# Attention and last feed-forward put into one block, with the first token blocks, the first products and the first gates rearranged

## The chip, the cores and the metric

The kernel runs on one core of a Trainium2 chip. The metric is the time of one execution on the device in microseconds, lower is better. Engines that run side by side, each in its own program order: TensorE (PE: matmuls and transposes), VectorE (DVE), ScalarE (ACT), GpSimd (POOL), and SyncE (SP), which here only issues DMAs. They wait for each other by semaphores. TensorE reads from SBUF and writes to PSUM, which has 8 banks of 2 KB per partition.

## What is computed

2048 tokens (16 blocks of 128) of width 256 go through two layers, each an attention and a feed-forward with a residual and a tanh gate. The change is in the second layer:

```python
x = x + tanh(g_xattn[1]) * L1_xattn(layernorm(x), ctx, ctx)      # 16 heads of 16, causal, 128 keys per block
x = x + tanh(g_ffn[1]) * L1_ffn(layernorm(x))

def L1_ffn(xf):                       # D = 256, hidden 128, E = 32 experts, 8 groups
    s = sigmoid(xf @ Wr.T + br)
    # best 4 of 8 groups by the sum of their top 2, then the best 6 experts in them
    w = s[idx] / sum(s[idx]) * 2.5    # the gates, 0 for the other experts
    moe = sum over e of gate[:, e] * (square(relu(xf @ W1[e].T)) @ W2[e].T)
    shared = square(relu(xf @ Ws1.T)) @ Ws2.T    # hidden 256
    return shared + moe
```

## The kernel before

Each phase is a block of its own (`nc.Block()`), with one program per engine and a barrier at its end. The change touches the last two: the attention (lines 1253 to 1456) and the call of `feed_forward` with tag "f1" (line 1458), which shares its code with the first layer's feed-forward "f0" (`gated` is true there).

**Precision.** Products are made of fp32 numbers split in two: `hi` is a rounded copy (ScalarE), `lo` the rest (a subtraction on VectorE or GpSimd), and a product is three matmuls (hi hi, hi lo, lo hi) for each half of 256: six matmuls of 128x512.

**The attention** has 64 steps n, four for each of the 16 token blocks b (t = n % 4 is the head group). TensorE's order in a step: `turned(n)` (four transposes of the shifted scores, line 1320), `scores(n + 2)` (three matmuls), `values(n)` (line 1331), and in some steps `query_turned` or `out_rows(b - 1)` (four transposes, line 1340). ScalarE: `out_copy` at t = 0, `probs(n)` (the exponential of what `turned` wrote), `query_copy`, `key_hi(n + 4)`, `query_normed`, `query_hi`. VectorE: `maxima(n + 1)`, `shifted(n + 1)`, and per block `inverse`, `scaled`, `residual` (line 1422), `moments`. GpSimd: `key_lo`, `query_lo`, a few small operations. `row_bank` (bank 7) and `x_bank` (bank 3) each serve one user at a time.

**The last feed-forward** has 34 weight units (2 shared, 32 experts), gone through twice (p = 0, 1), each time for two token blocks of 512 (s = 0, 1): 136 units K. Unit K's steps are `h_prod(K)` (TensorE, line 1017), `hidden(K)` (relu, ScalarE), `square(K)`, for experts `squared_y(K)` (times the gate row, VectorE, line 904), `y_hi(K)` (ScalarE, line 791), `y_lo(K)` (VectorE, line 880), `o_prod(K)` (TensorE, line 1046). TensorE's order is `h_prod(K + LA)`, `o_prod(K)` with LA = 2; ScalarE's `hidden(K)`, `y_hi(K - 1)`, `square(K)`; VectorE's `y_lo(K - 1)`, `squared_y(K)`, and `w_lo` every second unit. `h_prod` uses banks K % 3, `o_prod` adds up in banks 4 to 7.

Before its first product the block prepares token blocks m = 0 and 1: `normed` (VectorE), `transposed` (TensorE, line 1056), `x_hi`, `x_lo`, `logits_t` (router product, line 1065), its copy, `logits` (line 1072), `logits`' bias addition; `keep_clock` (line 110) fills TensorE meanwhile with 10 and 12 matmuls that nobody reads. Then come `sigmoid(0)` with a table load (ScalarE) and the routes `gates_of(0)` (VectorE, some 50 small operations from line 1219 to 1247), given out in three portions a unit before unit 3. `GATES_T` and `GATES_COPY` say at which unit TensorE turns the gates (`gates_t`, line 1080) and ScalarE copies them; SP stores them in DRAM (`store_gates`, line 724) and loads each expert's row back, spread over 128 partitions (`gate_rows`, line 720), into four slots G. Units 0 to 3 are shared and need no gate.

## Time and profile before

| | us |
|---|---|
| median of 3 runs | 973.37 |
| lowest, highest | 971.01, 975.56 |
| the profiled execution | 974.85 |
| its span in the profile | 972.7 |
| TensorE busy in it | 921.6 (95%) |
| VectorE, ScalarE, GpSimd busy | 603.9, 521.9, 190.1 |

The attention's steps run from about 417 to 544 us, the last feed-forward from 546 to the end. A timeline row gives the start, the duration, engine and line, output <- inputs, shapes, and in brackets how long the engine had been idle and who released it. Equal neighbouring instructions are merged (x4). The chain of waits is the path that ended last: each piece begins where what it waited for had ended.

### The profile page before, as it was taken

The numbers are of one execution on the slowest core, as the hardware profiler recorded it, in microseconds if no ns is written. First come the engines' busy times: TensorE is split into PE (matmuls) and PEld (weight loads), VectorE is DVE, ScalarE is ACT, GpSimd is POOL, SyncE is SP. The second block draws the span as 40 slices with busy tenths as digits, with TensorE's granted clock in tenths as the row PEclk, the third lists the DMA queues.
The fourth block names the chain that finished last, engine by engine and source line by source line (L and its number), as shares of the span: only waits on it lengthen the run. The fifth ranks groups of instructions, "written<-read, shape, count | busy, mean of one in ns | idle before, by whom it ended". The sixth has DMA issues, their size and how long they took to land. (4 is left out here: it accounts for less than half of the span.)

```text
span 972.7 us, 14048 instructions
## 1 busy us (share of the span) xinstructions
PE 921.6 (95%) x4776; PEld 733.5 (75%) x4776; DVE 603.9 (62%) x1411; ACT 521.9 (54%) x939; POOL 190.1 (20%) x162
## 2 busy tenths in 40 slices
PE   6799889999999999989999787999999999999997
PEld 5799768877788888756666655778788888888886
DVE  6677654455554565488888654565855556565554
ACT  3222043434443335468887344667666766666665
POOL 5899300000000002057787100000000000000000
PEclk8899999999999999999999898999999999999999
DMA  8100020332211432025554104444445344544443
GB/s 303 51 1 1 29 86 17 104 100 90 93 49 51 141 131 60 17 98 180 182 171 153 56 13 152 134 130 135 137 130 147 108 130 133 151 138 145 148 123 116
DMA packets 58535, 105.43 MB, mean 108 GB/s; under 512 B 7360, under 2 KB 13888, under 8 KB 58080
## 3 DMA queue, kind: packets, MB, share of 16 engines
q1 hardware_dynamic: 57744, 104.39, 33.9%
q8 instruction: 39, 0.64, 0.3%
q14 instruction: 32, 0.26, 0.1%
q10 hardware_dynamic: 720, 0.14, 0.1%
HBM read 102.08 MB, written 2.42 MB: 107 GB/s over the span
## 5 line engine op out<-in xcount | busy, mean ns | idle before, releaser
L880 DVE TENSOR_TENSOR ylof<-yf,yhif 128x512 fp32r<-128x512 f32 x200 | 138.2, 691 | 175.8 <-ACT yhif L791 175.4
L1017 PE MATMUL bank<-xhf,whif 128*128 128x512 f32 x528 | 212.4, 402 | 1.5 <-ACT rf L766 1.5
L1017 PE MATMUL bank<-xlf,whif 128*128 128x512 f32 x528 | 208.7, 395 | 0.0
L1017 PE MATMUL bank<-xhf,wlof 128*128 128x512 f32 x528 | 208.5, 395 | 0.0
L791 ACT ACTIVATE yhif<-yf 128x512 fp32r<-128x512 f32 x200 | 125.6, 628 | 89.3 <-DVE yf L893 82.5
L1046 PE MATMUL bank<-yhif,whif 128*128 128x512 f32 x400 | 160.0, 400 | 12.8 <-DVE ylof L880 12.7
L1046 PE MATMUL bank<-yhif,wlof 128*128 128x512 f32 x400 | 158.1, 395 | 0.0
L1046 PE MATMUL bank<-ylof,whif 128*128 128x512 f32 x400 | 157.2, 393 | 0.0
L768 ACT ACTIVATE rf<-bank 128x512 f32<-128x512 f32 x136 | 81.2, 597 | 124.7 <-PE bank L1017 123.9
L1017 PEld LDWEIGHTS bank<-xhf,whif 128*128 128x128 f32 x528 | 99.6, 189 | 24.5 <-ACT rf L766 1.9
L1017 PEld LDWEIGHTS bank<-xhf,wlof 128*128 128x128 f32 x528 | 99.7, 189 | 23.9
L1017 PEld LDWEIGHTS bank<-xlf,whif 128*128 128x128 f32 x528 | 99.8, 189 | 21.7
L1046 PEld LDWEIGHTS bank<-yhif,whif 128*128 128x128 f32 x400 | 75.4, 188 | 34.6 <-DVE ylof L880 18.1
L904 DVE TENSOR_TENSOR yf<-tf,Gf 128x512 f32<-128x512 f32 x128 | 87.6, 684 | 10.1 <-DMA Gf<-gates 10.1
L505 POOL TENSOR_TENSOR k_blocks_lo<-k_blocks_sb,k_blocks_hi 128x512 fp32r<-128x512 f32 x64 | 82.1, 1286 | 57.2 <-ACT k_blocks_hi L501 56.6
L1046 PEld LDWEIGHTS bank<-yhif,wlof 128*128 128x128 f32 x400 | 75.5, 189 | 18.1
L1046 PEld LDWEIGHTS bank<-ylof,whif 128*128 128x128 f32 x400 | 75.4, 189 | 17.2
L780 ACT ACTIVATE tf<-rf 128x512 f32<-128x512 f32 x128 | 79.5, 621 | 0.0
L766 ACT ACTIVATE rf<-bank 128x512 f32<-128x512 f32 x64 | 38.2, 597 | 75.8 <-PE bank L1017 75.7
L875 DVE TENSOR_TENSOR wlof<-wrawf,whif 128x512 fp32r<-128x512 f32 (+1 forms) x100 | 77.0, 770 | 1.3 <-ACT whif L759 1.3
L759 ACT ACTIVATE whif<-wrawf 128x512 fp32r<-128x512 f32 (+1 forms) x100 | 69.1, 691 | 0.7 <-DMA wrawf<-in_wu 0.7
L137 POOL TENSOR_TENSOR rstd<-vpe,mhalf 128x8 f32<-128x8 f32 (+2 forms) x8 | 13.2, 1648 | 243.2 <-DVE vpe L130 243.2
(133 smaller groups left out, 1215.4 us busy)
## 6 DMA issues: line engine op xcount, KB each, us to landing
Gf<-gates SPq DMA_DIRECT2D x160, 256.0 KB, 3.7
wrawf<-in_wu SPq DMA_DIRECT2D x68, 256.0 KB, 2.6
k_blocks_sb<-in_k_blk SPq DMA_DIRECT2D x64, 256.0 KB, 4.1
wrawf<-in_wu SPq DMA_DIRECT2D x32, 384.0 KB, 3.1
v_slot<-in_v_rows SPq DMA_DIRECT2D x16, 256.0 KB, 2.7
ctx_windows<-in_ctx_win SPq DMA_DIRECT2D x3, 1024.0 KB, 10.8
toeplitz<-in_kpad SPq DMA_DIRECT2D x4, 512.0 KB, 8.9
X<-in_x SPq DMA_DIRECT2D x4, 512.0 KB, 9.2
```

What stands on the lines that cost most here:

```text
L137: pool.tensor_tensor(rstd[:, bs], vpe[:, bs], mhalf[:, bs], ALU.pow).then_inc(done, 1)
L505: pool.tensor_tensor(K2[:, n % KR, :], KM[:, n % KLR, :], K1[:, n % KR, :].bitcast(F32), ALU.subtract).then_inc(s_k2, 1)
L759: act.activation(whi[:, Nu % S, :], wraw[:, Nu % S, :], ACT.Copy).then_inc(s_wh, 1)
L766: act.activation(r[:, K % S, :], bk(2 * K % 3), ACT.Silu).then_inc(s_ac, 1)
L768: act.activation(r[:, K % S, :], bk(K % 3), ACT.Relu).then_inc(s_ac, 1)
L780: act.activation(t[:, K % S, :], r[:, K % S, :], ACT.Square).then_inc(s_sq, 1)
L791: act.activation(yhi[:, K % S, :], y[:, K % S, :], ACT.Copy).then_inc(s_yh, 1)
L875: dve.tensor_tensor(wlo[:, Nu % S, :], wraw[:, Nu % S, :], whi[:, Nu % S, :].bitcast(F32), ALU.subtract).then_inc(s_wo, 1)
L880: dve.tensor_tensor(ylo[:, K % S, :], y[:, K % S, :], yhi[:, K % S, :].bitcast(F32), ALU.subtract).then_inc(s_yl, 1)
L904: dve.tensor_tensor(y[:, K % S, :], t[:, K % S, :], G[:, j % S, :], ALU.mult).then_inc(s_yd, 1)
L1017: last = pe.matmul(o, w_[:, Nu % S, wc], x_[:, c, xs], start=(m == 0), stop=(m == 5))
L1046: last = pe.matmul(acc(s)[:, c, :], w_[:, Nu % S, wc], y_[:, K % S, :], start=(n == 0 and m == 0), stop=(n == U - 1 and m == 2), skip_grou ...
```

## The change

The two blocks become one: the attention's programs go on with those of the feed-forward, without a barrier.

- **Token blocks 0 and 1 are prepared inside the attention**, in steps 40 to 63: `normed_row` on ScalarE (eight rows, steps 42 to 49), `transposed` in steps 48, 49, 56, 57 into `row_bank` and `x_bank`, `logits_t` in 52 and 60, `logits` in 54 and 62, `x_hi` and copies on ScalarE, `x_lo`, `router_lo` and `logits_copy` on VectorE, and waits on TensorE before `query_turned` and `out_rows` (which reuse the two banks). GpSimd makes one more `shifts`. `keep_clock` in f1 is gone.
- **The first weights** are loaded behind the last keys, `w_hi(0..3)` in ScalarE's steps 60 to 63, `w_lo(0..3)` on GpSimd.
- **The attention's last pieces** (values of step 63, `out_copy`, `out_rows`, the last rows on VectorE) stand among the first products.
- **LA = 4** first-layer products ahead; `y_hi`, `y_lo` stand LY = 3 units behind. `y_lo(0..3)` on GpSimd. The square is written to y and the gate multiplied in place (buffer t is gone), so `square(K)` now waits for `y_lo(K - 4)`.
- **The routes** of the first half are made in one piece on VectorE before unit 0's step.
- **The first three gates** (units 4, 5, 6) don't go through DRAM: TensorE spreads them (`gate_spread`, four transposes of a broadcast column each) into the bank that `h_prod(K + 1)` used, after unit 3. Gate rows from unit 7 on are loaded as before, from a store that SP issues at the same place (K = 3); the gates are copied at unit 7 instead of 4.

The diff, without the moves of whole functions:

```diff
-            LA = 1 if gated else 2
+            LA = 1 if gated else 4
+            LY = 0 if gated else 3
+            FIRST = 0 if gated else 4
+            SPREAD = 0 if gated else 3
...
-                GATES_COPY = tuple(k + LAG for k in GATES_T) if gated else (4, 4, KP_ - 14 + LAG, KP_ - 8 + LAG)
+            GATES_COPY = tuple(k + LAG for k in GATES_T) if gated else (7, 7, KP_ - 14 + LAG, KP_ - 8 + LAG)
...
+            def normed_row(act, m, j):
+                b = m * BPB + j
+                act.wait_ge(shift_sems[tag][1], SHIFT0[tag] + 1)
+                last = act.activation(xn[:, m % 2, j, :], X[:, b, :], ACT.Identity, bias=nshift[:, b:b + 1], scale=rstd[:, b:b + 1])
+                if j == BPB - 1:
+                    last.then_inc(s_n, 1)
...
+                    if j < SPREAD:
+                        return
                     sp.wait_ge(s_gst[blk % 2], 16 * (blk // 2 + 1))
...
+            def gpsimd(pool):
+                if not gated:
+                    for Nu in range(2, 4):
+                        w_lo(pool, Nu)
+                    for K in range(FIRST):
+                        y_lo(pool, K)
...
                 def square(K):
                     act.wait_ge(s_ac, K + 1)
-                            if shared(K):
                     if K >= S:
                         act.wait_ge(s_yl, K - S + 1)
-                                act.activation(t[:, K % S, :], r[:, K % S, :], ACT.Square).then_inc(s_sq, 1)
+                    act.activation(y[:, K % S, :], r[:, K % S, :], ACT.Square).then_inc(s_sq, 1)
...
-                                if K > 0:
-                                    y_hi(K - 1)
+                        if K >= LY:
+                            y_hi(K - LY)
+                        hidden(K)
                         square(K)
...
+                    dve.wait_ge(s_sq, K + 1)
+                    if j < SPREAD:
+                        dve.wait_ge(s_gb, j + 1)
+                        gate = bk((K + 1) % 3)
+                    else:
+                        dve.wait_ge(s_gl[j % S], gates_loaded(j))
+                        gate = G[:, j % S, :]
+                    dve.tensor_tensor(y[:, K % S, :], y[:, K % S, :], gate, ALU.mult).then_inc(s_yd, 1)
...
+                else:
+                    making = gates_of(0)
+                    next(making)
+                    tail.last_rows(dve)
+                    finish_route(making)
...
                         if K >= 3:
                             pe.wait_ge(s_ac, K - 2)
+                        if 0 <= K - 2 * NS - 4 < SPREAD:
+                            pe.wait_ge(s_yd, K - 2 * NS - 3)
...
+                def gate_spread(K):
+                    _, _, n, s = where(K)
+                    pe.wait_ge(s_gt, 1)
+                    pe.wait_ge(s_ac, K + 2)
+                    for j in range(BPB):
+                        row = gt[:, s * BPB + j, n - NS:n - NS + 1].broadcast_to((P, P))
+                        last = pe.transpose(bk((K + 1) % 3)[:, j * P:(j + 1) * P], row, ident[:])
+                    last.then_inc(s_gb, 1)
...
-                        keep_clock(pe, bk(0), 10)
...
+                else:
+                    h_prod(0)
+                    tail.values(pe, 4 * NB - 1)
+                    h_prod(1)
+                    tail.out_rows(pe, NB - 1)
...
+                    if K == 2 * NS - 1:
+                        for i in range(SPREAD):
+                            gate_spread(2 * NS + i)
...
+                        if n in (48, 56):
+                            pe.wait_ge(s_sc, b - 1)
+                            f1.transposed(pe, b // 2 - 6, 0, row_bank)
+                        if n in (49, 57):
+                            pe.wait_ge(s_qt, b + 2)
+                            f1.transposed(pe, b // 2 - 6, 1, x_bank)
```

**TensorE, from the attention's end to the first product, before.** A tile bank0 to bank3 holds two PSUM banks. xnf1 are the normed rows, xhf1 and xlf1 their split transposes, whif1 the weights.

```order
L1340 MATMUL bank3<-ident,o_t 128x128 [waits c_out_scaled,c_out_t_copied]
L1340 MATMUL bank3<-ident,o_t 128x128 x3
L1280 UNCONDITIONAL_BRANCH
L1007 UNCONDITIONAL_BRANCH [waits barrier_Pool_Activation_PE_DVE_SP_release]
L110 MATMUL bank0<-ident 128x128 x10
L1056 MATMUL bank2<-ident,xnf1 128x128 [waits f1_normed]
...
L110 MATMUL bank0<-ident 128x128 x12
L1065 MATMUL bank2<-xhf1,rwhf1 32x512 [waits f1_x_lo,f1_router_split]
...
L1056 MATMUL bank3<-ident,xnf1 128x128 [waits f1_normed]
...
L1072 MATMUL bank2<-ident,ltsf1 128x32 [waits f1_logits_t_copied]
L1072 MATMUL bank2<-ident,ltsf1 128x32 x3
L1017 MATMUL bank0<-xhf1,whif1 128x512 [waits f1_w_lo]
```

The same place now:

```order
L1370 MATMUL bank2<-ident,shifted_scores 128x128 [waits c_exp,c_shifted]
L1370 MATMUL bank2<-ident,shifted_scores 128x128 x3
L1078 MATMUL bank0<-xhf1,whif1 128x512 [waits f1_w_lo]
...
L1381 MATMUL bank3<-probs_t,v_slot 32x128 [waits c_exp]
...
L1078 MATMUL bank0<-xhf1,whif1 128x512 [waits f1_w_lo]
...
L1390 MATMUL bank3<-ident,o_t 128x128 [waits c_out_scaled,c_out_t_copied]
L1390 MATMUL bank3<-ident,o_t 128x128 x3
L1078 MATMUL bank1<-xhf1,whif1 128x512 [waits f1_w_lo]
```

The clock keeping, the preparation and the block's end between the last transposes of the scores and the first product are gone, and the last values and output rows stand behind products 0 and 1.

**TensorE, after unit 3's second-layer product, before.** gtf1 are the gates, yhif1 a unit's squared hidden values.

```order
L1046 MATMUL bank3<-yhif1,whif1 128x512 [waits f1_y_lo]
...
L1080 MATMUL bank1<-ident,gtf1 32x128 [waits f1_gates_ready]
L1080 MATMUL bank1<-ident,gtf1 32x128 x3
L1080 MATMUL bank1<-ident,gtf1 32x128 [waits f1_gates_t_copied,f1_gates_ready]
L1080 MATMUL bank1<-ident,gtf1 32x128 x3
L1017 MATMUL bank0<-xhf1,whif1 128x512 [waits f1_activated,f1_w_lo]
```

And now:

```order
L1111 MATMUL bank3<-yhif1,whif1 128x512 [waits f1_y_lo]
...
L1129 MATMUL bank1<-ident,gtf1 128x128 [waits f1_activated,f1_gates_ready]
L1129 MATMUL bank1<-ident,gtf1 128x128 x3
L1129 MATMUL bank0<-ident,gtf1 128x128 [waits f1_activated,f1_gates_ready]
L1129 MATMUL bank0<-ident,gtf1 128x128 x3
L1129 MATMUL bank0<-ident,gtf1 128x128 [waits f1_activated,f1_gates_ready]
L1129 MATMUL bank0<-ident,gtf1 128x128 x3
L1120 MATMUL bank1<-ident,gtf1 32x128 [waits f1_gates_ready]
L1120 MATMUL bank1<-ident,gtf1 32x128 x3
L1120 MATMUL bank1<-ident,gtf1 32x128 [waits f1_gates_t_copied,f1_gates_ready]
L1120 MATMUL bank1<-ident,gtf1 32x128 x3
L1078 MATMUL bank1<-xhf1,whif1 128x512 [waits f1_y_done,f1_activated,f1_w_lo]
```

Three sets of spread transposes come in, the third of which waits for `f1_activated` of unit 7, and the gate transposes for the DRAM copy stand behind them, before the next product.

**VectorE, from the routes' end, before.** The line 904 operation is `squared_y`, 880 is `y_lo`, 875 `w_lo`.

```order
L1247 TENSOR_SCALAR gtf1<-wt1 128x256 [waits f1_route_step]
L880 TENSOR_TENSOR ylof1<-yf1,yhif1 128x512 [waits f1_y_hi]
L875 TENSOR_TENSOR wlof1<-wrawf1,whif1 128x512 [waits f1_w_hi]
L880 TENSOR_TENSOR ylof1<-yf1,yhif1 128x512 [waits f1_y_hi]
L904 TENSOR_TENSOR yf1<-tf1,Gf1 128x512 [waits f1_y_hi,g_loaded0,f1_squared]
L880 TENSOR_TENSOR ylof1<-yf1,yhif1 128x512 [waits f1_y_hi]
L904 TENSOR_TENSOR yf1<-tf1,Gf1 128x512 [waits f1_y_hi,g_loaded1,f1_squared]
L875 TENSOR_TENSOR wlof1<-wrawf1,whif1 128x512 [waits f1_w_hi]
L880 TENSOR_TENSOR ylof1<-yf1,yhif1 128x512 [waits f1_y_hi]
```

And now (966 is `squared_y`, 731 `y_lo`, 726 `w_lo`):

```order
L1319 TENSOR_SCALAR gtf1<-wt1 128x256 [waits f1_route_step]
L129 BN_AGGR mv<-stats 128x2 [waits c_moments_done]
...
L132 TENSOR_SCALAR vpe<-mv 128x8 [waits f1_moments]
L966 TENSOR_TENSOR yf1<-yf1,bank1 128x512 [waits f1_gate_spread,f1_squared]
L966 TENSOR_TENSOR yf1<-yf1,bank0 128x512 [waits f1_gate_spread,f1_squared]
L726 TENSOR_TENSOR wlof1<-wrawf1,whif1 128x512 [waits f1_w_hi,f1_w_lo]
L966 TENSOR_TENSOR yf1<-yf1,bank0 128x512 [waits f1_gate_spread,f1_squared]
L731 TENSOR_TENSOR ylof1<-yf1,yhif1 128x512 [waits f1_y_hi,f1_y_lo]
L966 TENSOR_TENSOR yf1<-yf1,Gf1 128x512 [waits g_loaded3,f1_squared]
L726 TENSOR_TENSOR wlof1<-wrawf1,whif1 128x512 [waits f1_w_hi]
L731 TENSOR_TENSOR ylof1<-yf1,yhif1 128x512 [waits f1_y_hi]
```

The first gated unit that waits for a loaded row was the first of all, and is now the fourth (g_loaded3, unit 7); unit 5's `y_lo` stands behind it.

## Rows read from the trace of the kernel before

**Rows 1.** Stretches: us, each engine's busy us (instructions), granted clock, DMA share, GB/s.
```profile
510.00:520.00 10.00, 9.97 (x88) 6.42 (x87) 8.37 (x16) 8.20 (x17) 7.69 (x7) 1.00 0.44 146
...
580.00:590.00 10.00, 3.63 (x20) 2.39 (x18) 0.69 (x1) 2.24 (x5) 0.00 (x0) 0.96 0.47 145
...
590.00:600.00 10.00, 9.18 (x30) 7.36 (x31) 6.38 (x12) 5.76 (x12) 0.00 (x0) 0.70 0.31 107
...
610.00:640.00 30.00, 30.00 (x136) 23.66 (x134) 17.45 (x31) 19.43 (x37) 0.00 (x0) 1.00 0.44 132
```

**Rows 2.** Timeline of TensorE: start us, us, line, operation, idle before and its releaser.
```profile
541.41 0.60 PE L1320 MATMUL bank<-ident,shifted_scores 128*128 128x128 f32 x4
...
543.85 0.66 PE L1340 MATMUL bank<-ident,o_t 128*128 128x128 f32 x4 [0.72 <-ACT o_t L1379]
...
590.82 0.79 PE L1046 MATMUL bank<-yhif,whif 128*128 128x512 f32 x1 [6.42 <-DVE ylof L880]
...
598.80 0.40 PE L1046 MATMUL bank<-yhif,whif 128*128 128x512 f32 x1
```

**Rows 3.** Chain that ended last, 540 to 600 us: start us, us, what, line.
```profile
556.38 0.45 PE bank L1056 x4
558.88 1.58 PE bank L1017 x6
562.49 1.28 ACT L815
564.24 0.27 DVE hi L1219
566.98 0.69 DVE ylof L880
567.67 0.60 DVE wlof L875
572.97 0.69 DVE ylof L880
576.14 0.61 DVE ylof L880
583.04 0.60 ACT gtsf L821
583.66 0.31 SPq L724
584.48 4.12 DMA Gf<-gates
597.57 1.39 PE bank L1017 x6
```

**Rows 4.** One line's instructions, lines 505, 512, 1422: duration min/median/max in ns.
```profile
L505 POOL TENSOR_TENSOR k_blocks_lo<-k_blocks_sb,k_blocks_hi x64: 1265/1281/1470, 376.4 to 535.9; 128x512 fp32r<-128x512 f32 x64
...
L512 ACT ACTIVATE xn_c<-X,neg_mean_scaled,rstd x16: 584/590/592, 363.2 to 518.2; 128x256 f32<-128x256 f32 x16
...
L1422 DVE SCALAR_TENSOR_TENSOR X<-o_norm,tg,X x16: 483/485/1069, 435.3 to 545.3; 128x256 f32<-128x256 f32 x16
```

**Rows 5.** Timeline of TensorE in the attention, the transposes of steps 50 and 54.
```profile
516.54 0.66 PE L1320 MATMUL bank<-ident,shifted_scores 128*128 128x128 f32 x4
...
524.22 0.66 PE L1320 MATMUL bank<-ident,shifted_scores 128*128 128x128 f32 x4
```

**Rows 6.** Waits of ScalarE, 410 to 541 us: us in total, times, longest.
```profile
ACT probs_t L1373 <- PE bank L1320: 26.3, 47, 1.6
```

**Rows 7.** Timeline of TensorE in the last feed-forward, products with waits before them.
```profile
690.47 0.40 PE L1046 MATMUL bank<-yhif,whif 128*128 128x512 f32 x1
...
704.48 0.40 PE L1017 MATMUL bank<-xhf,whif 128*128 128x512 f32 x1
...
960.89 0.40 PE L1046 MATMUL bank<-yhif,whif 128*128 128x512 f32 x1
...
964.98 0.50 PE L1046 MATMUL bank<-yhif,whif 128*128 128x512 f32 x1 [0.34 <-DVE ylof L880]
```

1241 lines of the change are left out of this document (661 added, 580 removed).

## The prediction

> **What bounds the kernel now.** I read the page's engine slices first, then the stretch table, because the change touches only the last 560 us. In the attention (510 to 520) TensorE is busy 9.97 us in 10 at full clock, and in the last feed-forward (610 to 640) 30.00 in 30 [rows 1]. So both stages are TensorE-bound, and only three things can change the time: TensorE work added or removed, its idle time, and its clock. The idle time sits between them: 3.63 busy in 10 at 580, and at 590 a clock of 0.70 [rows 1].
>
> The chain of waits tells what fills that hole. After the attention's last transposes (start 543.85, [rows 2]) come a block change, the clock-keeping matmuls, the preparation of token blocks 0 and 1, and only at 558.88 the first product [rows 2, 3]. Then the routing on VectorE holds the first units until 576.14, and then the gates' trip through DRAM (transposes, copies, a store, a load of 4.12 us) holds TensorE until 590.82 [rows 2, 3].
>
> For the sum I mark one span. It starts with the transposes of the last attention step (63) at 541.41, and ends at 598.80, where 9 first-layer and 6 second-layer products are done and all runs steadily [rows 2]: **57.4 us**. I call a set of six matmuls a product; it takes 1.39 us at full clock [rows 3]. What comes after is 257 products, the same in both kernels.
>
> **The change, part by part.**
>
> *1. The new start, with times counted from the start of step 63's transposes.* Prices: product 1.39 and its result 0.16 later (first ones 1.58 with it), a ScalarE 128x512 operation about 0.6 (0.52 to the next start), a VectorE one 0.6 to 0.7, table load 1.28, a set of four transposes 0.45, gate copy 0.6 [rows 3]; a GpSimd 128x512 subtraction 1.28 [rows 4].
> TensorE: transposes to 0.5, product 0 to 1.9, values(63) to 2.2, product 1 to 3.6. out_rows(15) wants ScalarE's out_copy, which stands behind the last exponential, w_hi(3), the table load and the sigmoid: ready at 3.95, so 0.4 idle; then products 2, 3, 4 to 8.7.
> The second-layer product of unit 0 needs y_lo(0), now on GpSimd: y_hi(0) ends at 7.9, plus 1.28, so 9.3 (0.7 idle). From there TensorE alternates without a wait (GpSimd delivers units 1, 2, 3 at 10.9, 12.6 and 16.2, each before it is wanted) and ends unit 3 at 19.05.
> The routes: 576.14 - 564.24 = 11.9 us in the old trace, less the other VectorE work inside it, 0.6 + 0.7 at 566.98 and 0.6 at 572.97, leaves 10 us [rows 3]. The new ones start at 3.5, with 2 us of last_rows among them: ready at about 15.5, under TensorE's products. That wait goes.
> What is late next is in the order at unit 3: three sets of spread transposes, then both gate transposes, then product 8. spread(6) wants relu(7), which stands on ScalarE behind y_hi(4), which wants squared_y(4) on VectorE, which wants spread(4). From 19.65: 0.7 + 0.65 + 0.6 brings relu(7) to 21.55, so 1.6 idle. The second gate transpose waits for the first's copy, 0.75 idle, and its own copy ends at 24.4.
> From there the old trace gives the road to a gate row in SBUF: the copy ended 583.64, the store's issue 583.66 to 583.97, the load's issue 584.48, its end 588.6 [rows 3]. In the old kernel the first load waited for the first store alone; unit 7 is of the second block and waits for the second store, which I put at 2.15 us from its issue (the first store had landed when the load was issued at 584.48, some 2 us after the first gate copy). So 24.4 + 2.15 + 4.15 = 30.7. VectorE is in order: squared_y(7) waits for that row, and behind it stand w_lo(5) and y_lo(5), which TensorE wants for unit 5's second product. 30.7 + 0.6 + 0.6 + 0.7 = **32.65**. TensorE is at that product at 27.75, so it idles 4.9 us. Spreading three gates only moves the DRAM wait from unit 4 to unit 7; it doesn't hide it.
> At 32.65, 15 products are done, as at 598.80. After the old idle of 6.42 us the clock was low for the first products: the stretch 590 to 600 has 0.70, and the four products from 590.82 to 598.80 took 7.98 us instead of 5.56 [rows 1, 2]. That is 2.4 over; I put it on the new idle too (nothing if the clock holds). New span: 35.1. **Gain 57.4 - 35.1 = 22.3** (20 to 25).
>
> *2. The attention carries the preparation.* TensorE gets 4 sets of 4 transposes (0.45 by the row, to 0.5), 2 logit products (six 128x512 matmuls each, so 1.39) and 2 small sets of transposes (below 0.45, I take 0.35) [rows 3]: 2.0 + 2.8 + 0.7 = 5.5 us, all on the path, since four steps take 524.22 - 516.54 = 7.68 us with no idle [rows 5]. ScalarE gets 8 normed rows of 0.59 [rows 4], 4 x_hi, 2 copies, a router copy, 4 w_hi (these in place of key copies that have ended). Its slack is the 26.3 us that it waits for TensorE in 47 waits, 0.56 a step [rows 6]. Steps 42 to 47 get a row each and no TensorE work; where a block begins (44), four operations stand in ScalarE's step already, and there the row lands in full. Over the six steps that is 1.0 to 2.0 over: I take 1.7. VectorE is busy 8.37 in 10 [rows 1], 1.25 us free per four steps; its 4 x_lo come in two pairs of 1.3 (the router and logit operations are small): 0.5 over. GpSimd's extra small operation delays a key block: I allow 0.3. The new waits ahead of out_rows and query_turned hold TensorE, and behind it stand the next transposes; by the step's rows x_lo ends as TensorE arrives, so nothing, or 0.3 at each of eight. Together **8.0 lost** (5.5 to 11).
>
> *3. Later.* While VectorE made the second route, the nine products from 690.47 to 704.48 took 14.01 us instead of 12.5 [rows 7]. Those stalls go, since a second-layer product now comes three units behind its square: **1.5**. At the end the last two second-layer products waited for y_lo; the last started at 964.98 where 960.89 + 2 x 1.39 = 963.67 was possible [rows 7]. Now four products (5.6 us) stand between the last first-layer product and the last second-layer one, over a chain of about 3.3: **1.3**. The in-place square adds a wait of ScalarE for y_lo of four units ago; behind it stand relu and y_hi, but TensorE is 4 ahead and wants relu three products later. Nothing, if so.
>
> *4. GpSimd's eight subtractions.* One row bears on a cost of them: residual, a VectorE operation on SBUF inputs beside GpSimd's key work, took 483 to 485 ns but once 1069 [rows 4]. The Trainium skill's page SBUF — State Buffer (Who interferes with whom) says that VectorE with two SBUF inputs and a GpSimd operation that reads SBUF exclude each other for a whole instruction. The trace agrees in one instance of 16. Its result here is rival C.
>
> **Sum.** 22.3 + 1.5 + 1.3 - 8.0 = 17.1. The profiled execution took 974.85 (span 972.7), 1.5 over the median of 973.37; so 957.7 in its terms, and **956.3** by the median.
>
> **Rivals.**
> A, the forecast: 956.3, own range 951 to 961.
> B, the attention pays more: ScalarE is full at a step's head, each operation added there delays an exponential, and TensorE waits for it. If all 15 (8 rows, 4 x_hi, 3 copies, about 8.4 us) land on the path beside TensorE's 5.5, the loss is 15, not 8: 963.3. For it: ScalarE's waits are only half a microsecond each [rows 6]; against: the operations stand mostly in steps where TensorE has added work too.
> C, GpSimd and VectorE exclude each other: the four y_lo of 1.28 run while the routes' small operations do; 4 x 1.28 = 5.1 brings the gates to 20.6, 1.6 after TensorE wants them: 957.9. Against: 15 of 16 rows show nothing.
> D, slower: the new coupling square - y_lo - y_hi through one buffer y stalls each unit. Its price is that of the nearest stall, 0.34 us before 964.98 [rows 7], at every second of 132 units: 22.4 lost, so 978.7. It decides from 17.1/132 = 0.13 us per unit. Against: the ring of four units has 11 us for some 3 us of work.
> E, more is won: the clock holds after the shorter idle (2.4) and the attention hides ScalarE's part (2): 951.9.
> That the change doesn't do what it says is no likely case: the order shows the preparation inside the attention, and no barrier.
>
> **Chances.** A 0.50, B 0.20, C 0.10, E 0.14, D and kin 0.06. Range 949.5 to 965, which leaves out D and the worst of B. Half a percent, about what a measurement of this kernel can tell from no change, is 4.9 us: faster 0.92, same 0.04, slower 0.04.
>
> **What would show it.** The stretch from step 63's transposes to product 15 at 35 us; one idle of about 5 us before unit 5's second product, ended by VectorE's y_lo behind a gate load; the span from attention step 40 to 63 longer by 8; steady units at 2.78 us; no VectorE stall before the last products. I am wrong if the steady units are longer, if the gate load isn't the last thing waited for, or if the attention grows by over 11.

## The result, and the profile after

| kernel | median us | ratio to before, 95% interval | span | step 40 starts | steps 40 to 63 | step 63 to the end |
|---|---|---|---|---|---|---|
| before | 972.72 | | 972.7 | 497.51 | 43.90 | 431.3 |
| after | 956.47 | 0.9824 [0.9806, 0.9842] | 953.6 | 494.99 | 50.80 | 407.8 |
| after, again | 957.22 | 0.9817 [0.9794, 0.9839] | 955.5 | 496.51 | 50.83 | 408.2 |

The forecast was 956.3, the time is 956.47. The last four columns are of the profiled execution: its span, the start of step 40's transposes in the attention, from there to step 63's transposes, and from there to the end of the span. The same four columns are given for every experiment below, since they tell more than the medians. All kernels of this study have the same instructions ahead of step 40, yet it begins anywhere from 494.8 to 498.3. So the difference of the two spans, 19.1, holds 2.5 us of a run's own variation, and the change is -23.5 behind step 63 and +6.9 in the attention: 16.6, against 16.25 by the medians.

Stretches of the changed kernel (as in [rows 1]):

```profile
510.00:520.00 10.00, 9.82 (x90) 6.47 (x88) 8.50 (x17) 9.82 (x20) 6.96 (x6) 1.00 0.39 131
560.00:570.00 10.00, 7.58 (x44) 6.03 (x43) 7.00 (x21) 4.96 (x9) 2.93 (x2) 1.00 0.00 1
570.00:580.00 10.00, 5.67 (x23) 4.32 (x22) 3.33 (x7) 4.08 (x7) 0.00 (x0) 0.85 0.64 197
580.00:590.00 10.00, 10.00 (x39) 7.96 (x38) 5.54 (x10) 5.35 (x10) 0.00 (x0) 0.81 0.41 132
610.00:640.00 30.00, 30.00 (x137) 23.82 (x136) 20.02 (x34) 22.08 (x39) 0.00 (x0) 1.00 0.45 139
```

The hole between the stages has shrunk. TensorE is busy 5.67 in 10 at its worst, where before it was 3.63 [rows 1], and the granted clock falls less far, to 0.81 where it was 0.70. ScalarE in the stretch 510 to 520 of the attention went up to 9.82 busy in 10, from 8.20. The new start on TensorE's timeline (as in [rows 2]); its time 0, the transposes of step 63, is the first row:

```profile
545.79 0.66 PE L1370 MATMUL bank<-ident,shifted_scores 128*128 128x128 f32 x4
...
567.71 0.62 PE L1129 MATMUL bank<-ident,gtf 128*128 128x128 f32 x4 [1.65 <-ACT rf L850]
...
578.62 0.80 PE L1111 MATMUL bank<-yhif,whif 128*128 128x512 f32 x1 [4.33 <-DVE ylof L731]
...
581.35 0.63 PE L1078 MATMUL bank<-xhf,whif 128*128 128x512 f32 x1
...
583.89 0.42 PE L1111 MATMUL bank<-yhif,whif 128*128 128x512 f32 x1
```

Unit 5's second-layer product (line 1111) begins at 578.62 - 545.79 = 32.83; the prediction had 32.65. The two products from 578.62 to 583.89 take 5.27 us in place of 2.77, without a gap between them: the low clock costs 2.5. The chain of waits of the same place (start, us, what; as in [rows 3]):

```profile
566.98 0.59 ACT rf L850
...
568.80 0.59 ACT gtsf L887
...
570.16 0.59 ACT gtsf L887
...
570.78 1.63 DMA gates<-gtsf
...
572.42 4.16 DMA Gf<-gates
...
576.67 0.69 DVE yf L966
577.37 0.60 DVE wlof L726
577.97 0.61 DVE ylof L731
```

Second gate copy, store, load, squared_y(7), w_lo(5), y_lo(5): the chain is the forecast's, piece by piece. Where it was off, two misses met: the copy ended at 24.97 instead of 24.4, and the store took 1.63 instead of 2.15.

### The profile page after: what moved, and what is told of

It is laid out like the page before. It is cut to its first block, busy times and chain, and to the rows that moved or that the text cites. A ratio compares the mean times of both kernels' runs of the same rounds, so it can differ in the third digit from the quotient of the medians.

```text
span 953.6 us, 13986 instructions
## 1 busy us (share of the span) xinstructions
PE 910.1 (95%) x4744; PEld 723.5 (76%) x4744; DVE 605.7 (64%) x1396; ACT 545.4 (57%) x947; POOL 200.7 (21%) x171
## 4 chain that ended last, share of the span: by engine, by line
PE 49%; DVE 3%; ACT 2%; issue 1%; DMA 1%; POOL 0%; DVEq 0%; SPq 0%; ACTq 0%; POOLq 0%
PE bank L1111 19%; PE bank L1078 18%; PE bank L1370 3%; PE bank L1381 2%; PE bank L1363 1%; PE bank L1362 1%; PE bank L1358 1%; PE bank L1390 1%; PE bank L534 1%; PE bank L770 1%; DVE X L668 0%; DMA Gf<-gates 0%; DVE shifted_scores L1560 0%; PE bank L752 0%; DVE max L1554 0%
## 5 line engine op out<-in xcount | busy, mean ns | idle before, releaser
L966 DVE TENSOR_TENSOR yf<-yf,Gf 128x512 f32<-128x512 f32 x125 | 86.5, 692 | 129.3 <-ACT yf L856 122.1
L731 DVE TENSOR_TENSOR ylof<-yf,yhif 128x512 fp32r<-128x512 f32 x196 | 134.4, 687 | 30.0 <-ACT yhif L867 29.7
L856 ACT ACTIVATE yf<-rf 128x512 f32<-128x512 f32 x136 | 86.0, 632 | 8.1 <-DVE ylof L731 3.7
L726 DVE TENSOR_TENSOR wlof<-wrawf,whif 128x512 fp32r<-128x512 f32 (+1 forms) x96 | 74.7, 778 | 12.7 <-ACT whif L722 5.6
L139 POOL TENSOR_TENSOR rstd<-vpe,mhalf 128x8 f32<-128x8 f32 (+2 forms) x8 | 13.2, 1647 | 232.2 <-DVE vpe L132 232.2
```

The costliest lines, as they stand in the source:

```text
L726: eng.tensor_tensor(wlo[:, Nu % S, :], wraw[:, Nu % S, :], whi[:, Nu % S, :].bitcast(F32), ALU.subtract).then_inc(s_wo, 1)
L731: eng.tensor_tensor(ylo[:, K % S, :], y[:, K % S, :], yhi[:, K % S, :].bitcast(F32), ALU.subtract).then_inc(s_yl, 1)
L856: act.activation(y[:, K % S, :], r[:, K % S, :], ACT.Square).then_inc(s_sq, 1)
L966: dve.tensor_tensor(y[:, K % S, :], y[:, K % S, :], gate, ALU.mult).then_inc(s_yd, 1)
```

## Experiments

In each diff, - is the changed kernel and + the experiment. All times of stretches are from the profiled executions, in the order of the table above.

| kernel | median us | ratio, interval | span | step 40 | 40 to 63 | 63 to end |
|---|---|---|---|---|---|---|
| e1_gates_first | 950.72 | 0.9766 [0.9740, 0.9792] | 948.3 | 495.26 | 50.81 | 402.2 |
| e2_no_spread | 958.76 | 0.9838 [0.9816, 0.9860] | 956.6 | 497.88 | 50.82 | 407.9 |
| e3_split_route | 956.80 | 0.9815 [0.9789, 0.9841] | 953.5 | 496.02 | 50.80 | 406.7 |
| e4_light_attention | 959.05 | 0.9854 [0.9832, 0.9877] | 957.1 | 496.84 | 53.17 | 407.1 |
| e5_y_lo_vector | 965.95 | 0.9922 [0.9891, 0.9953] | 963.5 | 494.79 | 50.80 | 417.9 |
| e7_prep_behind | 966.07 | 0.9916 [0.9892, 0.9940] | 960.9 | 494.94 | 44.38 | 421.6 |
| e8_new_start | 948.61 | 0.9745 [0.9722, 0.9767] | 946.2 | 495.77 | 50.80 | 399.6 |
| e9_best | 948.09 | 0.9728 [0.9704, 0.9751] | 943.8 | 495.30 | 50.12 | 398.4 |
| e10_two_ahead | 960.51 | 0.9844 [0.9817, 0.9871] | 957.8 | 498.28 | 50.78 | 408.7 |

**Is the gates' way through DRAM the last thing waited for?**

```diff
-            GATES_T = (...) if gated else (3, 3, KP_ - 14, KP_ - 8)
-            GATES_COPY = (...) if gated else (7, 7, KP_ - 14 + LAG, KP_ - 8 + LAG)
+            GATES_T = (...) if gated else (-1, -1, KP_ - 14, KP_ - 8)
+            GATES_COPY = (...) if gated else (6, 6, KP_ - 14 + LAG, KP_ - 8 + LAG)
...
                         h_prod(K + LA)
+                    if not gated and K == 3:
+                        gates_t(0)
                     o_prod(K)
+                    if not gated and K == 3:
+                        gates_t(1)
```

> The two transposes that make the DRAM copy of the gates go ahead of the three first gates that TensorE spreads (the first behind first-layer product 7, the second behind unit 3's output product), and ScalarE's two gate copies one unit earlier. In the changed kernel TensorE stood 4.33 us at unit 5's output product, behind a chain that begins with the second gate copy at 570.16 us and runs over the store, the load at 572.42 us, squared_y(7), w_lo(5) and y_lo(5); it also stood 0.77 us for the copy. Theory 1 (the gates' way through DRAM is the last thing that the new start waits for): the chain begins 3 to 4 us earlier, the 4.33 us fall to about 1 to 2 us and the 0.77 us go, while the gates of TensorE come no sooner than their transposes allow: 3.7 to 6.2 us less than the changed kernel, 950.3 to 952.8 us. Theory 2 (the wait for unit 5 is ended by work of VectorE that would be late anyway, its portions of the second route and its lower halves): within 1 us of the changed kernel, 955.5 to 957.5 us.

TensorE's waits, e1:

```profile
568.86 0.62 PE L1129 MATMUL bank<-ident,gtf 128*128 128x128 f32 x4 [1.65 <-ACT rf L850]
...
575.69 0.50 PE L1111 MATMUL bank<-yhif,whif 128*128 128x512 f32 x1 [1.71 <-DVE ylof L731]
```

The 4.33 fell to 1.71, the 0.77 before the second gate transposes is gone, and step 63 to the end takes 402.2 in place of 407.8. Theory 1 holds. So the DRAM chain bounds the changed kernel's start. Of the 5.6 us won, 3.4 are idle time of TensorE (1.65, 0.77 and 4.33 became 1.65 and 1.71), and the other 2.2 go to the clock, which cost 2.5 in the changed kernel and keeps its full value in e1's stretches:

```profile
570.00:580.00 10.00, 8.22 (x35) 6.04 (x34) 7.07 (x14) 5.76 (x11) 0.00 (x0) 1.00 0.54 190
580.00:590.00 10.00, 10.00 (x49) 8.25 (x48) 6.23 (x10) 7.32 (x14) 0.00 (x0) 1.00 0.50 159
```

**What do the spread gates bring?**

```diff
-            SPREAD = 0 if gated else 3
+            SPREAD = 0
...
-            GATES_COPY = (...) if gated else (7, 7, KP_ - 14 + LAG, KP_ - 8 + LAG)
+            GATES_COPY = (...) if gated else (6, 6, KP_ - 14 + LAG, KP_ - 8 + LAG)
```

> None of the first gates is spread on TensorE: the transposes for the DRAM copy come first, every gate comes through DRAM, and ScalarE's two gate copies go one unit earlier; all else as in the changed kernel. Theory 1 (spreading three gates on TensorE only moves the wait for DRAM from unit 4 to unit 7, as the prediction put it, and costs three transposes and ScalarE rows on the way): the time is that of the changed kernel within 1.5 us, 955 to 958 us, with one long wait of TensorE, about 6 to 9 us, at an earlier unit (output product 1 or 2) in place of those at units 5 and 3. Theory 2 (the spread gates are themselves a good part of the gain, since they keep TensorE busy for three units while DRAM is under way): 4 to 8 us slower than the changed kernel, 960 to 964 us.

TensorE's longest wait, e2:

```profile
577.81 0.79 PE L1078 MATMUL bank<-xhf,whif 128*128 128x512 f32 x1 [7.92 <-DVE wlof L726]
```

One wait of 7.92 takes the place of 1.65 and 4.33. It stands before a first-layer product, not at output product 1 or 2 as expected: the product wants w_lo, which stands behind the first two gate products. Step 63 to the end takes 407.9 where the changed kernel takes 407.8 and 408.2. The spread gates bring nothing in this order: theory 1. The median, 958.76, misses its range and would have told the wrong story; the whole difference lies ahead of step 40, which begins 2.9 us later than in the first profile of the changed kernel.

Beside e1 this says more. The first load of gate rows is issued 22.66 us behind step 63's transposes in e2, 22.55 in e1 and 26.63 in the changed kernel. So the three sets of spread transposes, standing ahead of the gate transposes, put the DRAM chain off by 4 us and gave back as much by filling the wait. Where the chain begins equally early, the spread gates are worth 402.2 against 407.9, 5.7 us.

**What stalls TensorE beside the second route?**

```diff
             for b in range(2 * BPB):
                 last = dve.match_replace(rd[:, b, :], m8[:, b, :], pd[:, b, :], TAKEN)
+                if halves and b == BPB - 1:
+                    yield
...
-                yield from top_k(dve, step, self.pd, self.rd, self.m8, E1, TOP1)
+                yield
+                yield from top_k(dve, step, self.pd, self.rd, self.m8, E1, TOP1, True)
...
+                yield
                 step(dve.tensor_tensor(self.wt[:], self.wt[:], self.sc[:], ALU.mult))
+                yield
                 step(dve.tensor_reduce(self.sm[:], self.wt[:], AX_X, ALU.add))
+                yield
...
                 step(dve.reciprocal(self.rc[:], self.sm[:]))
+                yield
```

> VectorE's work on the routes of the second half is handed out in smaller portions between the units' lower halves (five more places where it is left, one of them within the choice of experts); the same instructions in the same order among themselves. The prediction let the stalls beside the second route go (1.5 us) because first-layer products are made further ahead; the trace shows 0.21, 0.42 and some lengthened waits there, about 1.2 to 1.4 us in all, as before. Theory 1 (the stall is a portion of the route that stands on the in-order VectorE ahead of the lower half of an output, and no distance between first-layer products and units helps against it): 1 to 1.5 us less than the changed kernel, 955.0 to 955.5 us, and the waits near 680 and 687 us are gone from the trace. Theory 2 (the stall is from elsewhere, ScalarE's share or GpSimd beside VectorE): 0 to 0.3 us less, with the waits at the same units.

The changed kernel, TensorE's waits in the steady part:

```profile
681.52 0.50 PE L1111 MATMUL bank<-yhif,whif 128*128 128x512 f32 x1 [0.21 <-DVE ylof L731]
...
687.74 0.50 PE L1111 MATMUL bank<-yhif,whif 128*128 128x512 f32 x1 [0.42 <-DVE ylof L731]
```

and its VectorE ahead of the second of them:

```profile
684.53 0.42 DVE L1311 TENSOR_TENSOR wt<-rd,pd 128x256 f32<-128x256 f32 x1
684.98 0.42 DVE L1312 TENSOR_TENSOR wt<-wt,sc 128x256 f32<-128x256 f32 x1
685.44 0.42 DVE L1313 TENSOR_REDUCE sm<-wt 128x8 f32<-128x256 f32 x1
...
686.34 0.42 DVE L1316 TENSOR_TENSOR wt<-wt,rc 128x256 f32<-128x256 f32 x1
...
687.00 0.68 DVE L731 TENSOR_TENSOR ylof<-yf,yhif 128x512 fp32r<-128x512 f32 x1
```

A portion of the route, 2.5 us long without a gap, stands ahead of the lower half that TensorE waits for. With the portions cut, the timeline lists no wait of TensorE between 590 and 948, and from step 63 to the end of the last output product it takes 400.31 in place of 401.53: 1.22 less, of which 1.14 are lengthened products near 680 and 687 that are of normal length now: theory 1. The medians (956.80 to 956.47) don't show it, since executions of this kernel lay between 952.41 and 958.60.

**Can the attention carry the preparation for less?**

```diff
-                            shifts(pool, "f1", 0)
...
-                        if 42 <= n < 50:
-                            f1.normed_row(act, (n - 42) // 4, (n - 42) % 4)
+                        if n in ROWS:
+                            f1.normed_row(act, ROWS[n] // 4, ROWS[n] % 4)
...
+                        if n == 41:
+                            dve.wait_ge(deviation_sems["f1"][2], 1)
+                            dve.wait_ge(shift_sems["f1"][0], SHIFT0["f1"] + 1)
+                            dve.tensor_tensor(nshift[:, part_of("f1", 0)], nmean[:, part_of("f1", 0)], rstd[:, part_of("f1", 0)],
+                                              ALU.mult).then_inc(shift_sems["f1"][1], 1)
```

> Inside the attention, the shift of the second feed-forward's first quarter is made by VectorE at step 41 in place of GpSimd, and ScalarE's eight normed rows stand at steps 43, 45, 46, 47, 49, 51, 54 and 55 in place of 42 to 49, one to a step. In the changed kernel steps 43 to 47 are 1.1 us longer than before (TensorE waits 0.6 us for key halves of GpSimd in step 43), the steps to which TensorE's own preparation was added 5.9 us longer. Theory 1 (the helpers' part of the attention's growth is where the small instructions stand, and can be avoided; TensorE's part can't): 0.7 to 1.1 us less, 955.4 to 955.8 us, steps 43 to 47 as long as before, steps 48 to 62 as in the changed kernel. Theory 2 (any added instruction of ScalarE or VectorE lengthens an attention step, wherever it stands): the growth moves to the later steps and the time is the same within 0.3 us.

VectorE's timeline at step 42, e4, and GpSimd's:

```profile
502.21 1.23 DVE L1598 TENSOR_TENSOR neg_mean_scaled<-neg_mean,rstd 128x8 f32<-128x8 f32 x1 [2.63 <-POOL rstd L139]
```

```profile
500.54 1.63 POOL L139 TENSOR_TENSOR rstd<-vpe,mhalf 128x8 f32<-128x8 f32 x1
```

Both theories miss, because the experiment made a new wait. VectorE stood 2.63 us for GpSimd's power (L139), with the scores of step 43 behind it, so that step 42 took 4.63 us in place of 2.19, and step 43 took 3.42 in place of 3.18. The half on the rows can be read behind that: steps 44 and 45 are back at 1.64 and 1.70, from 1.79 and 1.98, and of the later ones only step 52 grew, from 3.06 to 3.18. That is 0.43 off at steps 44 and 45 and 0.12 back.

**What do GpSimd's subtractions cost and bring?**

```diff
-                    for K in range(FIRST):
-                        y_lo(pool, K)
...
                     variances(dve, tag, 1)
+                    for K in range(FIRST):
+                        y_lo(dve, K)
```

> The lower halves of the first four outputs are made by VectorE, behind all of its route, in place of GpSimd beside it. It measures two things. First, what GpSimd's four instructions cost the route: in the changed kernel the route ended at 17.5 us of the new start where 15.5 were worked out, and two short VectorE instructions lasted 1.34 and 0.98 us beside GpSimd's, where such instructions last about 0.2. Theory 1 (GpSimd holds VectorE up): without it both last 0.2 us and the route ends at 15.4 to 15.8. Theory 2 (the route is late for another reason): it ends at 17 or later. Second, what the place buys: unit 0's output product then waits for the route, at 16 to 18 us in place of 9.4, and everything behind it is 6.5 to 8.5 us later: 963 to 965 us.

Two lines of the route in the changed kernel (duration min/median/max in ns, first and last start), then GpSimd's timeline beside them:

```profile
L1306 DVE TENSOR_TENSOR pd<-sc,gm x4: 258/266/1342, 555.6 to 557.2; 128x64 f32<-128x64 f32 x4
...
L1314 DVE TENSOR_SCALAR sm<-sm x1: 978/978/978, 561.3 to 561.3; 128x8 f32<-128x8 f32 x1
```

```profile
555.52 1.30 POOL L731 TENSOR_TENSOR ylof<-yf,yhif 128x512 fp32r<-128x512 f32 x1 [0.39 <-ACT yhif L867]
...
560.96 1.29 POOL L731 TENSOR_TENSOR ylof<-yf,yhif 128x512 fp32r<-128x512 f32 x1 [2.41 <-ACT yhif L867]
```

The same two lines in e5:

```profile
L1306 DVE TENSOR_TENSOR pd<-sc,gm x4: 262/265/274, 555.4 to 555.9; 128x64 f32<-128x64 f32 x4
...
L1314 DVE TENSOR_SCALAR sm<-sm x1: 170/170/170, 560.1 to 560.1; 128x8 f32<-128x8 f32 x1
```

Without GpSimd beside them, 1342 ns become 274 at most and 978 become 170. The route ends at 15.67 of the new start, where the prediction had 15.5 and the changed kernel has 17.52. So GpSimd holds VectorE up for 1.85 us, all of it at these two instructions: theory 1. And unit 0's product starts at 17.08 in place of 9.41, in the expected range, but all behind it is 10.1 later (417.9 to 407.8), more than the 6.5 to 8.5. TensorE's timeline in e5 shows why:

```profile
562.67 0.80 PE L1111 MATMUL bank<-yhif,whif 128*128 128x512 f32 x1 [8.21 <-DVE ylof L731]
...
565.39 0.63 PE L1078 MATMUL bank<-xhf,whif 128*128 128x512 f32 x1
...
567.19 0.40 PE L1111 MATMUL bank<-yhif,whif 128*128 128x512 f32 x1
...
588.59 0.79 PE L1111 MATMUL bank<-yhif,whif 128*128 128x512 f32 x1 [5.17 <-DVE ylof L731]
```

Unit 0's product is 7.67 later. Unit 1's, at 567.19, followed it after 4.52 us instead of 2.88, and TensorE had no idle time between them: after the idle 8.21 us the granted clock was 0.50, the lower of its two levels (stretch 563 to 565), which cost 1.64. The wait at unit 5's product is 0.84 longer than the changed kernel's 4.33, since the load of the gate row took 5.01 us in place of 4.16. Together 10.15.

The coupling of rival D shows in ScalarE's timeline of e5:

```profile
562.71 0.63 ACT L854 ACTIVATE yf<-rf 128x512 f32<-128x512 f32 x1 [6.97 <-DVE ylof L731]
```

square(4) stood 6.97 us for y_lo(0), since y has a ring of four, and y_hi(2) stood behind it. TensorE didn't feel it: y_lo(2) was done at 564.58, and its product began only at 569.97, without a wait.

**What is the preparation inside the attention worth?** Undone: transposes, halves and logits of token blocks 0 and 1 stand behind the attention, with VectorE's normed rows.

```diff
-                        if n in (48, 56):
-                            pe.wait_ge(s_sc, b - 1)
-                            f1.transposed(pe, b // 2 - 6, 0, row_bank)
...
+                    tail.values(pe, 4 * NB - 1)
+                    tail.out_rows(pe, NB - 1)
+                    for m in range(2):
...
+                        for c in range(2):
...
+                            transposed(pe, m, c, prep_bank(m, c))
...
+                    logits(pe, 0, prep_bank(0, 1))
                     h_prod(0)
-                    tail.values(pe, 4 * NB - 1)
+                    logits_t(pe, 1, prep_bank(1, 0))
+                    logits(pe, 1, prep_bank(1, 1))
                     h_prod(1)
-                    tail.out_rows(pe, NB - 1)
```

> The preparation of the first two token blocks (transposes, halves, logits) is put back behind the attention, with its banks and VectorE's normed rows as in the kernel before; first-layer products four ahead, the spread gates, GpSimd's lower halves and the common block stay. It measures what the part inside the attention is worth on net. Theory 1 (the prediction's sum: the attention pays, by the trace 6.9 us, and the start gains the length of the preparation): the attention's steps 40 to 63 take 43.9 us as before, the route and with it the first gates are 9 to 12 us later, and the whole is 2 to 6 us slower than the changed kernel, 958.5 to 962.5 us. Theory 2 (the products four ahead and the four shared units cover a late route, so that its place hardly matters): as fast or faster than the changed kernel, 950 to 957 us.

TensorE's waits in e7, 539 to 590 (us in total, times, longest), those of the preparation:

```profile
PE bank L783 <- ACT ltsf L778: 1.9, 2, 1.2
PE bank L770 <- DVE xlf L762: 1.7, 1, 1.7
...
PE bank L752 <- DVE xnf L982: 1.3, 1, 1.3
```

The attention takes 44.38 and the rest 421.6: 6.4 less and 13.8 more than in the changed kernel, 7.4 slower on net (9.6 by the medians; the profiled execution lies 3.1 below the median of this kernel). That is beyond the 2 to 6 of theory 1, and theory 2 is out. The route ends 11.4 us later, within the expected 9 to 12, at 28.95 of the new start, but it isn't the bound: the gates are wanted only at 33.1. What is late is TensorE itself, by its own work of the preparation, 5.86 us by the steps of the attention that carry it in the changed kernel, and by 4.9 us of waits between its links, which the attention covers with other work. Of the remaining 3 us, 1.1 are other waits on balance (0.69 and 0.72 at step 63's values and out_rows, which the changed kernel covers with products 0 and 1, 0.43 more at unit 0's product, 0.72 less at unit 5's). The clock cost another 1.5: a router product from 546.47 on took 2.54 us instead of 1.39 and a first-layer product from 577.57 on 2.59 instead of 1.47, against 0.82 less behind unit 5's wait. A second finding: without the preparation the attention is still 0.48 longer than before, with step 43 at 2.93 in place of 2.48. GpSimd's added shift is all that is left there.

**Can the start be freed of DRAM?** On top of e1:

```diff
-                        if K >= LY:
+                        if K >= LY and K != 7:
                             y_hi(K - LY)
                         hidden(K)
+                        if K == 7:
+                            y_hi(4)
...
+                        if K - LY == FIRST:
+                            dve.wait_ge(s_yl, FIRST)
+                            y_lo(dve, 4)
+                            w_lo(dve, 5)
+                            y_lo(dve, 5)
+                            y_lo(dve, 6)
...
+                        if K == 4:
+                            dve.wait_ge(s_wo, 4)
+                            w_lo(dve, 4)
                         squared_y(K)
```

> The earlier gate transposes of the first experiment, and on top of them the order around the first gates from DRAM: VectorE makes the lower weight halves of wave 4 ahead of its first product with a gate, and the lower halves of units 4, 5 and 6 and of weight wave 5 ahead of squared_y(7), which waits for DRAM; ScalarE takes relu(7) ahead of the upper half of unit 4. In the first experiment TensorE still stood 1.65 us at the third spread gate for relu(7) and 1.71 us at unit 5's output product for the lower half behind squared_y(7). Theory 1 (both are waits of order on an in-order engine, nothing of their own needs the gate from DRAM): both go, unit 5's product starts at 26.3 to 27.5 us of the new start in place of 29.6, and the time is 2.2 to 3.4 us below the first experiment's 950.7, 947.3 to 948.5 us. Theory 2 (the DRAM gates are still the bound, one or two units later): the wait comes back at unit 6 or 7 and the time is that of the first experiment within 1 us.

TensorE's waits over 0.1 us from unit 1 on, e8, and its stretch 570 to 580:

```profile
568.08 0.62 PE L1136 MATMUL bank<-ident,gtf 128*128 128x128 f32 x4 [0.37 <-ACT rf L850]
...
577.79 0.63 PE L752 MATMUL bank<-ident,xnf 128*128 128x128 f32 x4 [0.44 <-DVE xnf L979]
```

```profile
570.00:580.00 10.00, 9.50 (x43) 7.44 (x43) 7.02 (x15) 6.21 (x12) 0.00 (x0) 1.00 0.60 207
```

Unit 5's product starts at 26.45, and no wait for a gate is left. The stretch behind step 63 is 2.6 shorter than e1's: theory 1. The median, 948.61, is 2.1 below e1's and misses the expected range by 0.1.

**All together**

```diff
-                        if n == 4 * 10:
+                        if n == 39:
                             deviations(pool, "f1", 0)
+                        if n == 40:
                             shifts(pool, "f1", 0)
```

with e3's portions, e8's start and e4's rows.

> The start of e8_new_start, the route in smaller portions (in the trace of that experiment alone 1.24 us less from step 63 on), and the lighter attention in another form: GpSimd's inverse deviations at step 39 and its shift at step 40, each in a gap of the key halves, ScalarE's rows one to a step as in that experiment. There the shift on VectorE stood 2.63 us for GpSimd's power of the deviations and made step 42 2.4 us longer. Theory 1 (parts add up; GpSimd's shift and power cost only where they stand ahead of key halves that TensorE waits for): steps 40 to 63 take 49.4 to 50.0 us in place of 50.8, and the whole is 1.9 to 2.7 us below e8_new_start, 944.8 to 946.4 us if that gives 947.9. Theory 2 (the attention's growth can't be moved): 1.2 us below it.

The two stretches together take 448.5 in place of e8's 450.4 and the changed kernel's 458.6. Steps 40 to 63 take 50.12, just outside the 49.4 to 50.0: step 43 went from 3.18 to 2.14, step 45 from 1.98 to 1.70, but step 42 from 2.19 to 2.71, where TensorE now waits 0.33 for a key block behind GpSimd's power of the deviations. The median of 948.09 misses the expected range, and is no clear gain over e8's 948.61; the executions lay between 945.81 and 949.12. Against the kernel before it is 0.9728 [0.9704, 0.9751], against the changed one some 8 to 9 us less (956.47 and 957.22), which is faster than both.

**What do four products ahead bring?** From e2:

```diff
-            LA = 1 if gated else 4
-            LY = 0 if gated else 3
+            LA = 1 if gated else 2
+            LY = 0 if gated else 1
...
-            GATES_COPY = (...) if gated else (6, 6, KP_ - 14 + LAG, KP_ - 8 + LAG)
+            GATES_COPY = (...) if gated else (4, 4, KP_ - 14 + LAG, KP_ - 8 + LAG)
```

> The experiment without spread gates, with the products of the first layer two ahead instead of four and upper halves one unit behind instead of three, as in the kernel before; the preparation stays in the attention. It measures what four ahead gives by itself. Theory 1 (every gate waits for the same chain of route, transposes, store and load, which begins behind unit 3's output product; with four ahead TensorE has two more first-layer products behind it when it comes to stand, so 2 x 1.385 = 2.8 us of work lie inside the wait): from the start of step 63's transposes to the last output product it takes 2.3 to 3.3 us more than the 394.4 us of the experiment without spread gates, 396.7 to 397.7. Theory 2 (two ahead reaches unit 3's output product 2.8 us earlier, the chain begins earlier by as much where the route is ready, and nothing is lost): 394 to 395.5 us. Theory 3 (the distance is what keeps lower halves ahead of the products in the steady part): over 399 us, with waits at many units.

The 394.4 of the expectation is the start of the last five output products, which stand without a first-layer product between them; here only three do, so its number doesn't compare. Counted to the end of the last output product it is 401.62 in e2 and 402.64 in e10: 1.0 more, below theory 1's range and within theory 2's. TensorE's waits behind the start, e10:

```profile
688.54 0.50 PE L1111 MATMUL bank<-yhif,whif 128*128 128x512 f32 x1 [1.02 <-DVE ylof L731]
...
950.04 0.50 PE L1111 MATMUL bank<-yhif,whif 128*128 128x512 f32 x1 [0.70 <-DVE ylof L731]
```

At the start nothing is lost. Unit 3's product begins at 15.67 instead of 17.84, the gate transposes follow 1.8 earlier, and the chain through DRAM with them. What four ahead brings is the end of the kernel (0.7) and 0.4 beside the second route.

**The changed kernel again**

> The changed kernel once more, beside the other on the same chip. The parts before step 40 are the same instructions in all kernels of this study, yet step 40 began between 494.8 and 497.9 us of the profiled executions. Theory 1 (a run's first 120 us vary with the granted clock around the first matmuls and with nothing of the change): its stretches from step 40 to 63 and from step 63 to the last output product repeat within 0.2 us (50.8 and 394.3), and the time lies between 955.5 and 959 us. Theory 2 (the start is a property of each program): step 40 again at 495.0 within 0.3 us.

50.83 and 401.85 (to the end of the last output product; 401.53 the first time), and step 40 at 496.51 instead of 494.99: theory 2 is out. Theory 1 holds for the attention (0.03), but behind step 63 the two differ by 0.32, more than its 0.2: the wait at unit 5's product is 4.49 instead of 4.33. The stretch 105 to 125 us, in turn before, after and e10:

```profile
105.00:125.00 20.00, 15.59 (x110) 14.53 (x110) 13.32 (x51) 2.15 (x4) 5.42 (x4) 0.91 0.22 79
```

```profile
105.00:125.00 20.00, 14.62 (x113) 13.02 (x112) 13.27 (x49) 3.52 (x7) 4.74 (x4) 1.00 0.28 97
```

```profile
105.00:125.00 20.00, 15.59 (x103) 14.97 (x102) 12.00 (x47) 2.15 (x4) 5.19 (x4) 0.83 0.22 78
```

The granted clock there is 0.91, 1.00 and 0.83, and step 40 comes at 497.51, 494.99 and 498.28. It is not the only such place: the repeated run has 0.91 there too and 496.51, and in the stretch 40 to 60 the clock is 0.92 before and 0.97 after.

## Why the prediction was right, point by point

- **What bounds the kernel.** Right. TensorE is busy 9.82 in 10 and 30.00 in 30 in the two stages, and all that changed is its added work, its idle time and its clock.
- **The new start, gain 22.3.** Right, 22.1: unit 5's product at 32.83 for 32.65, and 2.5 for the clock where 2.4 was taken. Within it the route ends at 17.52, not 15.5. The step that missed it laid GpSimd's subtractions at nothing beside VectorE; e5 shows 1.85 us. It cost nothing, because the gates are wanted only at 19.2. So rival C's mechanism is real, at 1.85 of the 5.1 us that it was given, and its price was hidden. The subtractions at 553.86 and 557.20 cost it nothing: the match and MAX8 instructions beside them lasted as long as in e5. The Trainium skill's page SBUF — State Buffer (Who interferes with whom) says that a tensor_scalar can take the shared ports too, in one of its modes, and that a tensor_reduce can't. The trace agrees with the first: the tensor_scalar was stretched to 978 ns. For the second it has one instance, which agrees: the tensor_reduce ahead of it (560.85, 0.42 us in both kernels) had begun when the same GpSimd subtraction did (560.96), and that took 1.29 us, as long as those beside the match instructions (1.28).
- **"Spreading three gates only moves the DRAM wait."** Right for this order, and shown: e2 has the same time to 0.1 us behind step 63. But it is the order that makes it so: with the gate transposes first (e1) the same spread gates are worth 5.7 us.
- **The attention pays 8.0.** The mechanism was right, and the term too large: 6.9. The steps to which TensorE's own work was added (48, 49, 52, 54, 56, 57, 60, 62) grew by 5.86, where 5.5 was worked out. The helpers' part was put at 2.5 and is about 1.1: 0.70 at step 43, of which e7 gives 0.45 to GpSimd's shift, and 0.43 at steps 44 and 45. That and the other 0.25 go with ScalarE's rows: they are gone in e7, which has no rows there. How the place of a row decides isn't shown in full: with the same moved rows, step 44 takes 1.64 in e4 and 1.79 in e9. VectorE's 0.5 doesn't appear as a wait. Rival B is out, although ScalarE is now busy 9.82 in 10 in one stretch. Its 15 is 13.9 by the terms that it names, 8.4 and 5.5, and the attention pays half of that.
- **Second-route stalls, 1.5.** This step failed: 1.14 us of lengthened products remain of 1.51, so it brought 0.4. It said that the stalls go "since a second-layer product now comes three units behind its square". But VectorE works in order: squared_y(K) and y_lo(K - 3) are neighbours there, and a portion of the route ahead of the pair delays both. First-layer products moved ahead by two and upper and lower halves back by two, so by the order from a square to the product that wants its lower half there is no more room than before. e3 takes the stalls away by shorter portions, and they measure 1.22.
- **End of the kernel, 1.3.** Right: the last output product now starts without a wait (0.16 us of lengthened products remain, so 1.2 was won), and e10, two ahead, shows one of 0.70 there again.
- **Rival D, the coupling.** It costs nothing in the changed kernel, whose steady units take 2.78 us. ScalarE does stand for it where a lower half is very late, 3.74 us at 578.66 in the changed kernel and 6.97 in e5, but no wait of TensorE came from it in either.
- **The sum.** 22.1 + 0.4 + 1.2 - 6.9 = 16.8 by its parts, 16.6 by the stretches, 16.25 by the medians, forecast 17.1. That the total came so near is in part luck: two terms missed by 1.1 each with opposite sign. So is the 0.17 us between 956.3 and 956.47, which is less than the medians of one kernel differ by (956.47 and 957.22).

What stays open: 0.4 of e7's 13.8 us; and why the stretch behind step 63 varies between executions of the same instructions there, 407.1 in e4, 407.8 and 408.2 in the changed kernel. Most of it is how long the low clock lasts: the two products behind unit 5's wait took 4.35, 5.27 and 5.29 us.

## What to carry to other kernels

Follow a wait back through the in-order engines before moving more work under it: here the DRAM round trip was the bound, but what TensorE wanted (y_lo(5)) didn't need the gate from DRAM, it only stood behind an instruction that did. And start the longest chain first: three gates spread by hand brought nothing while they stood ahead of it, and 5.7 us once four lines of order had put them behind it. A distance between producer and consumer helps only if it grows on the engine that is late. And compare kernels by stretches between the same instructions, with the waits in them beside: a difference of 1 us that is lost in the medians can be read there.

## What the runs showed of the hardware that was not expected

- A single VectorE instruction on 8 elements of each partition lasted 978 ns beside a GpSimd subtraction, and 170 ns without it; both times in the changed kernel the stretched one ended within 0.15 us of GpSimd's end. In e7 the same instruction, with no subtraction beside it, lasted 0.17 us. MAX8 beside one of these subtractions lasted as long as without (0.84 us for eight).
- TensorE idled 6.75 us in three waits within 12.6 us of the changed kernel, and its next two products ran at about half speed. In e1 it idled 3.36 us in two, and the granted clock stayed at 1.00. In e5 one wait of 8.21 us was enough: the granted clock behind it was 0.50.
- The granted clock at 105 to 125 us, with the same instructions, was 0.83, 0.91 or 1.00 from one execution to the next, and the start of step 40 lay between 494.79 and 498.28 us.
